# Scattering 48 of the 68 early expert results later: kept in DRAM and scattered in the experts stage, 20 more after the gathers

## The chip, the cores and the metric

The kernel runs on one core of one Trainium2 chip. The metric is device time in microseconds: the median of three runs is 3254.08 us (3247.41 to 3254.96). The execution that was profiled took 3249.84 us, and its trace spans 3248.0 us.

## What is computed

A graph layer on N = 12500 nodes with D = 256 features and E = 212500 edges (sorted by their target), then a layer norm. Cut to what matters here:

```python
h = feats * rsqrt(deg_out)[:, None]
m = segment_sum(h[src], dst) * rsqrt(deg_in)[:, None]
x = m @ W_gc + b_gc + feats @ W_res + b_res
logits = x @ Wg + bg                       # 64 experts, top 2, softmax over the two
for each expert e, its nodes s:            # 256 -> 512 -> 256, gelu
    y[s] += gate * (gelu(x[s] @ w1[e] + b1[e]) @ w2[e] + b2[e])
y = x + y
out = (y - mean) * rsqrt(var + eps) * gamma + beta      # over the nodes
return layernorm(feats + out)                           # over the features
```

## The kernel before

There are four stages, each ended by a barrier over all engines: the columns of the graph and the degrees (to about 350 us of the trace), `aggregate` (to about 2394 us), `experts` (to about 3060 us), and `norms`. Nodes stand in NT = 98 tiles of 128, edges in chunks of 128, PER = 17 chunks to a tile.

**Aggregate** runs in 98 slots, one for a tile. In each, GpSimd (POOL) gathers the source rows of the slot's chunks from `h_table`, one indirect DMA of 128 rows for each chunk, 15 of 17 (L1582); the other two come from `x_ahead` by a plain DMA of SyncE's queue (SP). TensorE (PE) multiplies each chunk with a one-hot matrix into PSUM (L2154), and at fixed chunk numbers k of the slot does the steps of earlier tiles: the product with the weights (k = 3), ranks (13), turning (15), listing the places (16). POOL may be up to 24 chunks ahead of PE. VectorE (DVE) makes the one-hots and does the routing arithmetic.

From slot 63 to slot 96 each slot also computes two **early sets** (jobs 0 to 67): 128 nodes of one expert whose rows are complete in the first 56 tiles. For a job, SP loads the expert's weights (`load_expert`, 1,152 KB in four DMAs, L1425 to L1428), POOL gathers the 128 rows (`fetch_job`, L1556), and PE turns them and computes the hidden layer and the output: for the slot's first job at k = 0, 4 and 8, for its second at k = 8, 11 and 15. `keep_job_turned` (L1812) on DVE copies the turned rows that the hidden layer's matmuls (L2081) wait for. `finish_job` on DVE adds the bias to the output (L1819), makes the gate (L1820, L1822), scales into a ring buffer `eys` of EY = 6 results (L1828), and adds it to a total (L1830). Then POOL scatters the result into `picked` (`send_job`, L1565), each node's two expert results in DRAM.

What sets the order is each engine's own program. DVE's program of slot s ends with: `finish_job` of the slot's first job, `add_x1`, `add_beta` of tile s - 2 (L1650), `finish_job` of its second job; then slot s + 1 begins with routing (L1683 to L1714) and `keep_job_turned` of the first job. SP's program of slot s: a row of `x_ahead`, small columns for later jobs (L1415), weights of the first job of slot s + 1, then `load(s)`, which first waits for `add_beta(s - 2)` (`keep_x_beta`, L1382) and for the landing of what it stored (L1389), another row of `x_ahead` (L1393), in slots with s % 7 = 2 a clearing of part of `picked` (L1403, 1,792 KB) and a store of seven tiles of x1 (L1434, 903 KB), in slots with s % 7 = 6 a load of `m_base` (903 KB), and last the weights of the second job of slot s + 1.

**Experts** runs one turn for each remaining set of 128 nodes, 160 turns in this data. PE's turn is the hidden layer (L2442), turning the next rows (L2435) and the output (L2449). POOL's turn is one scatter of a result (`send`, L2305), which waits for DVE's scaled result (L2382), and one gather of the rows four turns on (`fetch`, L2298). At its start ACT's queue brings 56 tiles of x1 back into `acc3` (L2289), whose space the jobs had used.

## Time and profile before

| | us |
|---|---|
| runs | 3247.41, 3254.96, 3254.08; median 3254.08 |
| the profiled execution | 3249.84 |
| its span in the trace | 3248.0 |
| granted TensorE clock, mean | 0.935 of full speed |
| PE, PEld, DVE busy | 2667.9, 2037.5, 2056.3 |
| ACT, POOL busy | 1243.7, 2108.0 |

PE's busy time is its matmuls with modelled ends, PEld the weight loads beside them. An engine that is busy 82% of the span need not be what the time waits for, and one that is busy 65% may be: POOL's indirect DMAs have a fixed gap between them that counts as idle. What bounds a stage is read in that stage. The page's chain of work that ended last goes back only to the last stage, so it says nothing about the two stages that the change touches; these are read by the timeline and the waits.

### The profile page before, as it was taken

What the parts mean: (1) busy time and instruction counts of PE and PEld (TensorE: products, weight loads), DVE (VectorE), ACT (ScalarE), POOL (GpSimd) and SP (SyncE); (2) the same over time, 40 slices, a digit from 0 to 9 for tenths busy, and PEclk for the clock granted to TensorE, in tenths of its full rate; (3) what the DMA queues carried; (4) which work ended last, traced back from release to release, by engine and by line L of the source; (5) the groups of instructions that cost most, each with busy time, mean ns of one, the idle gap of its engine ahead of it and who ended that gap; (6) DMA issues with size and microseconds to landing.
All of it is one profiled execution on the core that took longest, in us unless ns stands there. A gap on an engine that the chain in (4) does not pass through costs nothing. (4 is left out here: it accounts for less than half of the span.)

```text
span 3248.0 us, 60035 instructions
## 1 busy us (share of the span) xinstructions
PE 2667.9 (82%) x14992; PEld 2037.5 (63%) x14993; DVE 2056.3 (63%) x7118; ACT 1243.7 (38%) x2934; POOL 2108.0 (65%) x2142
## 2 busy tenths in 40 slices
PE   4751689999999899888898989888959999999650
PEld 3541456565666566555776767676748888889640
DVE  7993356666666566666666666666655555555698
ACT  5991122222232232232433334333324444444339
POOL 6887677777777777777777777777714554555300
PEclk9885899999999999999999999999979999999885
DMA  8559545455554654556878787786766555554477
GB/s 259 158 177 342 183 138 180 146 177 188 149 177 144 191 178 143 181 171 188 256 240 255 239 252 242 241 261 214 235 231 189 175 182 181 187 174 138 148 290 248
DMA packets 415795, 653.48 MB, mean 201 GB/s; under 512 B 70847, under 2 KB 307165, under 8 KB 413938
## 3 DMA queue, kind: packets, MB, share of 16 engines
q1 hardware_dynamic: 299790, 355.25, 33.3%
q0 software_dynamic: 101712, 273.85, 28.3%
q10 hardware_dynamic: 14100, 22.04, 1.9%
q8 instruction: 93, 1.52, 0.2%
q14 instruction: 100, 0.82, 0.1%
HBM read 515.73 MB, written 139.19 MB: 202 GB/s over the span
## 5 line engine op out<-in xcount | busy, mean ns | idle before, releaser
L1582 POOL DMA_INDIRECT work<-h_table,src_cols x1452 | 1383.5, 953 | 453.9 <-issue 428.1
L2154 PE MATMUL ps<-work 128*128 128x257 f32 x3322 | 999.5, 395 | 132.0 <-DMA work<-h_table,src_cols 124.3
L2154 PEld LDWEIGHTS ps<-work 128*128 128x128 f32 x3322 | 574.3, 192 | 387.4 <-issue 262.4
L2305 POOL DMA_INDIRECT picked<-ys,places x160 | 170.7, 1067 | 269.1 <-DVE ys L2382 247.5
L1982 PE MATMUL ps<-none_w,none 128*128 128x512 bf16 x879 | 335.6, 382 | 0.0
L2442 PEld LDWEIGHTS ps<-xst,work 128*128 128x128 f32 x2560 | 310.8, 193 | 27.4 <-issue 17.8
L2442 PE MATMUL ps<-xst,work 128*128 128x128 f32 x2560 | 315.5, 277 | 12.6 <-issue 11.9
L2449 PE MATMUL ps<-work,hid 128*128 128x256 f32 x1280 | 307.5, 383 | 2.1 <-ACT hid L2284 1.0
L2284 ACT ACTIVATE hid<-ps,b_cols 128x128 f32<-128x128 f32 x640 | 218.2, 367 | 117.7 <-PE ps L2442 86.7
L2449 PEld LDWEIGHTS ps<-work,hid 128*128 128x128 f32 x1280 | 231.2, 191 | 35.8 <-ACT hid L2284 10.4
L1607 DVE TENSOR_TENSOR work<-rel_cols,ps 128x1152 f32<-128x1152 f32 x196 | 250.5, 1279 | 3.8 <-PE ps L2154 3.7
L1654 DVE TENSOR_TENSOR logits<-ps,gate_bias 128x64 f32<-128x64 f32 x98 | 22.0, 225 | 344.6 <-ACT acc L1489 344.6
L2298 POOL DMA_INDIRECT ring<-x_rows,rows_at x162 | 158.0, 975 | 100.2 <-issue 45.2
L1485 ACT ACTIVATE acc<-acc,f_in 128x256 f32<-128x256 f32 x98 | 49.9, 509 | 382.8 <-DVE f_in L1638 382.8
L1509 ACT ACTIVATE work<-work,f_ahead 128x256 f32<-128x256 f32 x182 | 92.8, 510 | 266.5 <-DMA work<-x_ahead 266.5
L878 ACT ACTIVATE stairs<-iota_f,work 128x128 bf16<-128x128 f32 x624 | 182.6, 399 | 6.0 <-PE ps L955 5.8
L1489 ACT COPY acc<-ps 128x256 f32<-128x256 f32 x98 | 36.5, 372 | 367.2 <-PE ps L2020 362.0
L2093 PE MATMUL ps<-acc 128*128 128x256 f32 x544 | 131.8, 385 | 42.4 <-ACT acc L1516 42.4
L2279 ACT COPY xs<-ring 128x256 f32 (+1 forms) x162 | 65.6, 405 | 250.7 <-POOLq L2325 243.9
L2397 DVE TENSOR_TENSOR ysum<-ps,work 128x256 f32<-128x256 f32 x160 | 68.0, 425 | 134.8 <-PE ps L2449 134.6
L2093 PEld LDWEIGHTS ps<-acc 128*128 128x128 f32 x544 | 100.7, 190 | 67.8 <-ACT acc L1516 55.3
L2081 PEld LDWEIGHTS ps<-acc 128*128 128x128 f32 x1088 | 134.4, 195 | 10.5 <-issue 7.1
(374 smaller groups left out, 5055.4 us busy)
## 6 DMA issues: line engine op xcount, KB each, us to landing
acc<-in_L_gnn_w_dram SPq DMA_DIRECT2D x136, 512.0 KB
work<-in_L_gnn_w_dram SPq DMA_DIRECT2D x128, 512.0 KB
picked<-work SPq DMA_DIRECT2D x14, 1792.0 KB
work<-x_ahead SPq DMA_DIRECT2D x182, 128.0 KB
pk<-picked SPq DMA_DIRECT2D x13, 1792.0 KB, 10.0
work<-h_table,src_cols POOLq DMA_INDIRECT x1452
acc<-m_base SPq DMA_DIRECT2D x14, 903.0 KB, 6.6
x_beta<-xr_x SPq DMA_DIRECT2D x98, 128.0 KB, 2.2
```

What stands on the lines that cost most here:

```text
L878: mm = nc.scalar.activation(stairs[:, k, n, :], iota_f[:, :], ACT.Sign, scale=-1.0, bias=lo_half[:, bass.ds(g * PIECES + 2 * WHOLE + n, 1)])
L1582: pool.indirect_dma_start(out=got[:, c % RING, 0:D], out_offset=None, in_=h_table[:, :], in_offset=bass.IndirectOffsetOnAxis(ap=src_cols[: ...
L1607: nc.vector.tensor_tensor(hot[:, (2 * t + h) % HOTS, 0:b - a, :], rel_cols[:, a:b].unsqueeze(2).broadcast_to([P, b - a, P]), lanes.unsquee ...
L1982: nc.tensor.matmul(ps[:, 7, :], none[:, :], none_w[:, :], start=False, stop=False)
L2081: mm = nc.tensor.matmul(ps[:, 4, h * P:(h + 1) * P], ew1[:, j % EW, k, h * P:(h + 1) * P], exst[:, k, :], start=(k == 0), stop=(k == KD - 1))
L2093: mm = nc.tensor.matmul(ps[:, 5, 0:D], ehid[:, h, :], ew2[:, j % EW, h, :], start=(h == 0), stop=(h == KH - 1))
L2154: mm = nc.tensor.matmul(ps_flat[:, bank(t, k, w[0])], hot[:, (2 * t + (k >= HALF)) % HOTS, k % HALF if k >= HALF else k, :], got[:, c % RI ...
L2284: nc.scalar.activation(hid[:, h, :], ps[:, h, 0:SUP], ACT.Gelu, bias=b1_cols[:, h, bass.ds(e, 1)]).then_inc(h_set, 1)
L2298: pool.indirect_dma_start(out=ring[:, u, :], out_offset=None, in_=x1_rows[:, :], in_offset=bass.IndirectOffsetOnAxis(ap=rows_at[:, u:u + 1 ...
L2305: pool.indirect_dma_start(out=picked[:, :], out_offset=bass.IndirectOffsetOnAxis(ap=places[:, u:u + 1], axis=0), in_=ys[:, u, :], in_offse ...
L2442: mm = nc.tensor.matmul(ps[:, h, 0:SUP], w1s[:, u, k, h * P:(h + 1) * P], xst[:, k, :], start=(k == 0), stop=(k == KD - 1))
L2449: mm = nc.tensor.matmul(ps[:, 4, 0:D], hid[:, h, :], w2s[:, u, h, :], start=(h == 0), stop=(h == KH - 1))
```

## The change

The results of the 68 jobs are no longer scattered between the gathers. Jobs 0 to 47 (`KEPT`) are stored by SP into a new DRAM table `y_jobs`, two per slot, at the end of SP's slot: the first job of the slot before, and the second job of two slots before. In the experts stage they are loaded back in six DMAs of ACT's queue, and POOL scatters one of them per turn in turns 8 to 55 (`send_kept`). The results of jobs 48 to 67 (`SENT_LAST` = 20) stay in SBUF, in `acc3` tiles 56 to 75 whose rows have been stored by then, and POOL scatters them after the last gather. The ring `eys` is 4 results instead of 6, and DVE's scaling waits for the store of the result four jobs before (`ey_out`) instead of the scatter of six jobs before (`ey_sent`). The tiles of x1 come back in 17 DMAs instead of 8: four from ACT's queue (tiles 50 to 55, and in three parts tiles 56 to 75, which held the late results), and from SP's queue twelve of four tiles and one of two, after the kept results that stood there were scattered. For this SP's loop over the experts' weights is unrolled, and so are 14 rounds of POOL's.

```diff
+y_jobs = nc.dram_tensor("y_jobs", [KEPT * P, D], F32).ap()
...
-        EW, ER, EY, EC = 3, 4, 6, JOBS
+        EW, ER, EY = 3, 4, 4
...
+        def y_of(j):
+            return eys[:, j % EY, :] if j < KEPT else acc3[:, COUNTED + j - KEPT, 0:D]
...
+                def store_job(j):
+                    if j >= KEPT:
+                        return
+                    sp.wait_ge(ey_set, j + 1)
+                    if j >= 2:
+                        sp.wait_ge(ey_out[j % 2], 16 * (j // 2))
+                    sp.dma_start(by_lane(y_jobs)[:, j, :], y_of(j)).then_inc(ey_out[j % 2], 16)
...
                     for j in jobs_in(slot + 1)[1:]:
                         load_expert(j)
+                    for j in jobs_in(slot - 1)[0:1]:
+                        store_job(j)
+                    for j in jobs_in(slot - 2)[1:]:
+                        store_job(j)
...
                     if c in fetch_at:
                         fetch_job(fetch_at[c])
-                    if c in send_at:
-                        send_job(send_at[c])
...
+                pool.wait_ge(zeros_out, 16 * SETS)
+                for j in range(KEPT, JOBS):
+                    send_job(j)
+                pool.wait_ge(ey_sent, 16 * SENT_LAST)
...
-                    if j >= EY:
-                        dve.wait_ge(ey_sent[j % 2], 16 * ((j - EY) // 2 + 1))
-                    nc.vector.tensor_scalar(eys[:, j % EY, :], eysum, egate[:, 1:2], None, ALU.mult).then_inc(ey_set, 1)
+                    if EY <= j < KEPT:
+                        dve.wait_ge(ey_out[j % 2], 16 * ((j - EY) // 2 + 1))
+                    elif j == KEPT:
+                        dve.wait_ge(rows_out, stored_to(COUNTED + SENT_LAST))
+                    nc.vector.tensor_scalar(y_of(j), eysum, egate[:, 1:2], None, ALU.mult).then_inc(ey_set, 1)
...
-                with sp.Fori(0, X // U - 1) as i:
+                for i in range(X // U - 1):
                     weights_ahead(i, U)
+                    q = i - QUADS_BARE
+                    if 0 <= q < KEPT_QUADS:
+                        for u in range(R):
+                            sp.wait_ge(kept_sent[u], 16 * (q + 1))
+                        x1_again(sp, *FREED[q + 1])
+                    if q == KEPT_QUADS - 1:
+                        x1_again(sp, *FREED[0])
...
-                for g in range(COUNTED // GT):
-                    act.dma_start(acc3[:, g * GT:(g + 1) * GT, :], by_lane(x1_rows)[:, g * GT:(g + 1) * GT, :]).then_inc(x1_back, 16)
+                for j in range(0, KEPT, PIECE):
+                    act.dma_start(kept[:, j:j + PIECE, :], by_lane(y_jobs)[:, j:j + PIECE, :]).then_inc(kept_in, 16)
+                for a, b in UNUSED:
+                    x1_again(act, a, b)
...
+                def send_kept(n, q, u):
+                    if n == 0:
+                        pool.wait_ge(kept_in, 16 * (KEPT // PIECE))
+                    if q > 0:
+                        pool.wait_ge(kept_sent[u], 16 * q)
+                    pool.indirect_dma_start(out=picked[:, :], out_offset=bass.IndirectOffsetOnAxis(ap=kept_columns[:, n, 1:2].bitcast(I32), axis=0),
+                                            in_=kept[:, n, :], in_offset=None, bounds_check=PLACES - 1,
+                                            oob_is_err=False).then_inc(kept_sent[u], 16)
...
                         if u < fetches:
                             fetch(u)
+                        if kept_quad is not None:
+                            send_kept(R * kept_quad + u, kept_quad, u)
```

SP in aggregate, one slot without a clearing, from `keep_x_beta` to the end of the slot; before:

```order
L1382 DMA x_beta<-xr_x 128x256 [waits any_gathered9]
L1389 DMA xr_x<-in_x_dram 128x256 [waits any_gathered12]
L1393 DMA work<-x_ahead 128x256 [waits any_turns_begun]
L1422 TENSOR_LOAD acc [waits hist_done_any]
L1425 ISA
L1425 DMA acc<-in_L_gnn_w_dram 128x2x512
L1426 DMA acc<-in_L_gnn_w_dram 128x4x256
L1427 ISA
L1427 DMA acc<-in_L_gnn_b_dram 128x256
L1428 ISA
L1428 DMA acc<-acc 128x4
L1393 DMA work<-x_ahead 128x256 [waits any_turns_begun]
```

and of the change (here the slot's end is the two stores, and the names in the brackets are of semaphores that share a number with others: `halves_set_any` is `ey_set`, `risen_set_any` and `col_counted_any` are `ey_out` of even and odd jobs):

```order
L1409 DMA xr_x<-in_x_dram 128x256 [waits any_gathered13]
L1413 DMA work<-x_ahead 128x256 [waits any_gathered0]
L1450 TENSOR_LOAD acc [waits hist_done_any]
L1453 ISA
L1453 DMA acc<-in_L_gnn_w_dram 128x2x512
L1454 DMA acc<-in_L_gnn_w_dram 128x4x256
L1455 ISA
L1455 DMA acc<-in_L_gnn_b_dram 128x256
L1456 ISA
L1456 DMA acc<-acc 128x4
L1443 DMA y_jobs<-acc 128x256 [waits risen_set_any,halves_set_any]
L1443 DMA y_jobs<-acc 128x256 [waits col_counted_any,halves_set_any]
```

The two stores to `y_jobs` stand behind the four DMAs of the weights of the next slot's second job.

DVE in aggregate, `add_beta` and `finish_job` of the second job of slot 65 (job 5); before:

```order
L1650 TENSOR_TENSOR xr_x<-xr_x,ag_beta_b 128x256 [waits any_hot_set]
L1819 TENSOR_TENSOR acc<-ps,acc 128x256 [waits halves_set_any,consts_set,hot_used_any]
L1820 TENSOR_TENSOR acc<-acc 128x1
L1822 SCALAR_TENSOR_TENSOR acc<-acc 128x1 [waits stairs_ready_any]
L1828 TENSOR_SCALAR acc<-acc 128x256 [waits hist_done_any,stairs_ready_any]
L1830 TENSOR_TENSOR acc<-acc 128x256 [waits halves_set_any]
L1720 TENSOR_TENSOR code_diag<-ident,ahead_hi 128x256 [waits f_turned_any]
L1683 SCALAR_TENSOR_TENSOR junk,rt_rank<-iota_f,picks,ps 128x64 [waits ranked]
```

and of the change:

```order
L1677 TENSOR_TENSOR xr_x<-xr_x,ag_beta_b 128x256 [waits any_summed]
L1846 TENSOR_TENSOR acc<-ps,acc 128x256 [waits halves_set_any,consts_set,hot_used_any]
L1847 TENSOR_TENSOR acc<-acc 128x1
L1849 SCALAR_TENSOR_TENSOR acc<-acc 128x1 [waits stairs_ready_any]
L1857 TENSOR_SCALAR acc<-acc 128x256 [waits col_counted_any,hist_done_any,stairs_ready_any]
L1859 TENSOR_TENSOR acc<-acc 128x256 [waits halves_set_any]
L1747 TENSOR_TENSOR code_diag<-ident,ahead_hi 128x256 [waits f_rows_set_any]
L1710 SCALAR_TENSOR_TENSOR junk,rt_rank<-iota_f,picks,ps 128x64 [waits ranked]
```

The order is the same; the scaling (L1828, now L1857) of job 5 has a new wait for the store of an odd job (`col_counted_any`), and stands right behind `add_beta` (L1650, now L1677). Before, this semaphore was that of the scatters, waited for from job 6 on.

POOL in experts, the first turns before (scatters L2305, gathers L2298):

```order
L2305 DMA picked<-ys,places 25088x256 [waits paced,tiles_set_any]
L2298 DMA ring<-x_rows,rows_at 128x258
L2305 DMA picked<-ys,places 25088x256 [waits zero_set,tiles_set_any]
L2298 DMA ring<-x_rows,rows_at 128x258
L2305 DMA picked<-ys,places 25088x256 [waits paced,hot_used_any,tiles_set_any]
L2298 DMA ring<-x_rows,rows_at 128x258
```

and from turn 8 of the change on (L2357 is `send`, L2350 `fetch`, L2377 `send_kept`; `f_out_set_any` is `kept_in`):

```order
L2357 DMA picked<-ys,places 25088x256 [waits paced,hot_used_any,tiles_set_any]
L2350 DMA ring<-x_rows,rows_at 128x258
L2377 DMA picked<-acc 25088x256 [waits f_out_set_any]
L2357 DMA picked<-ys,places 25088x256 [waits zero_set,hist_done_any,tiles_set_any]
L2350 DMA ring<-x_rows,rows_at 128x258
L2377 DMA picked<-acc 25088x256
L2357 DMA picked<-ys,places 25088x256 [waits paced,hot_used_any,tiles_set_any]
```

From turn 8 on a third indirect DMA follows the other two.

## Rows read from the trace of the kernel before

**Rows 1.** Windows: start:end us, length, busy us, clock, DMA share, GB/s.

```profile
1597.21:2125.14 527.93, 473.69 (x2533) 375.65 (x2531) 340.26 (x1281) 196.15 (x396) 400.96 (x417) 0.99 0.80 250
2125.14:2337.28 212.14, 191.97 (x1026) 151.75 (x1024) 134.94 (x513) 81.96 (x164) 161.26 (x168) 0.99 0.76 239
2440.00:3050.00 610.00, 587.98 (x3961) 537.56 (x3961) 335.39 (x1278) 269.78 (x764) 310.46 (x305) 1.00 0.54 169
```

**Rows 2.** Groups of POOL, 1597.21 to 2125.14: busy, mean ns, idle before.

```profile
L1582 POOL DMA_INDIRECT work<-h_table,src_cols x329 | 314.2, 955 | 100.2 <-issue 96.9 <-PE ps L2154 2.1 <-DVE acc L1828 1.2
L1565 POOL DMA_INDIRECT picked<-acc x44 | 44.7, 1015 | 13.4 <-issue 13.4
L1556 POOL DMA_INDIRECT acc<-x_early,acc x44 | 42.7, 970 | 13.4 <-issue 12.8 <-DVE acc L1828 0.6
```

**Rows 3.** Waits, 1597.21 to 2125.14: total us, times, longest.

```profile
PE ps L2154 <- DMA work<-h_table,src_cols: 20.0, 17, 3.8
```

**Rows 4.** Timeline of PE, two slots: start us, us, what, idle before.

```profile
1802.23 1.95 PE L2081 MATMUL ps<-acc 128*128 128x128 f32 x16
...
1815.65 1.99 PE L2093 MATMUL ps<-acc 128*128 128x256 f32 x8 [1.61 <-ACT acc L1516]
...
1824.69 1.95 PE L2081 MATMUL ps<-acc 128*128 128x128 f32 x16
```

**Rows 5.** Timeline of DVE around the same slot's end.

```profile
1814.42 0.42 DVE L1650 TENSOR_TENSOR xr_x<-xr_x,ag_beta_b 128x256 f32<-128x256 f32 x1
1817.68 0.42 DVE L1819 TENSOR_TENSOR acc<-ps,acc 128x256 f32<-128x256 f32 x1 [2.85 <-PE ps L2093]
...
1818.46 0.46 DVE L1828 TENSOR_SCALAR acc<-acc 128x256 f32<-128x256 f32 x1
...
1823.62 0.42 DVE L1812 COPY acc<-ps 128x256 f32<-128x256 f32 x1
```

**Rows 6.** Timeline of SP's queue there.

```profile
1814.87 0.36 SPq L1382 DMA_DIRECT2D x_beta<-xr_x  x1
...
1818.77 0.41 SPq L1425 DMA_DIRECT2D acc<-in_L_gnn_w_dram  x1
...
1820.41 0.53 SPq L1428 DMA_DIRECT2D acc<-acc  x1
```

**Rows 7.** DMA queues, 1818.5 to 1826.5: packets, MB, share of 16 engines.

```profile
q1 hardware_dynamic: 1383, 1.45, 57.0%
```

**Rows 8.** Timeline of DVE, slot 79.

```profile
1935.90 0.35 DVE L1828 TENSOR_SCALAR acc<-acc 128x256 f32<-128x256 f32 x1
```

**Rows 9.** Timeline of SP's queue, slot 79.

```profile
1942.53 1.38 SPq L1428 DMA_DIRECT2D acc<-acc  x1
```

**Rows 10.** Timeline of PE, slot 80.

```profile
1954.95 2.02 PE L2081 MATMUL ps<-acc 128*128 128x128 f32 x16 [0.51 <-DMA acc<-acc]
```

**Rows 11.** Windows: two slots, and the start of the experts.

```profile
1761.15:1789.44 28.29, 22.91 (x117) 17.90 (x115) 15.53 (x59) 8.92 (x18) 21.58 (x23) 0.94 0.89 290
1789.44:1811.89 22.45, 20.85 (x117) 16.95 (x115) 15.55 (x59) 8.92 (x18) 16.97 (x19) 1.00 0.80 253
...
2405.00:2408.00 3.00, 2.17 (x9) 1.78 (x10) 0.61 (x2) 0.40 (x1) 0.94 (x1) 0.50 0.98 362
2408.00:2411.00 3.00, 3.00 (x15) 2.91 (x15) 0.24 (x1) 1.41 (x4) 0.94 (x1) 0.50 1.01 401
```

**Rows 12.** DMA issues by line: KB each, median us to landing.

```profile
acc<-m_base SPq DMA_DIRECT2D x14, 903.0 KB, 6.6
x_beta<-xr_x SPq DMA_DIRECT2D x98, 128.0 KB, 2.2
```

**Rows 13.** Timeline of POOL in the experts.

```profile
2605.13 1.00 POOL L2305 DMA_INDIRECT picked<-ys,places  x1 [1.37 <-DVE ys L2382]
2606.44 0.98 POOL L2298 DMA_INDIRECT ring<-x_rows,rows_at  x1 [0.30 <-issue]
```

**Rows 14.** Timeline of POOL between the stages.

```profile
2397.85 0.99 POOL L2298 DMA_INDIRECT ring<-x_rows,rows_at  x1 [41.32 <-DVE rows_at L2358]
```

More of the change, by code:

```diff
@@ L43 @@
 PER_SLOT = 2
+JOBS = PER_SLOT * (JOB_LAST - JOB_FIRST + 1)
+SENT_LAST = 20
+KEPT = JOBS - SENT_LAST
+KEPT_TILE = 2
+QUADS_BARE = 2
+KEPT_QUADS = KEPT // 4
 GT = 7
@@ L1479, in _ @@
                 sp.wait_ge(rows_out, 16 * (ALL_IN + SETS - 1 + SET))
+                for n in range(2):
+                    sp.wait_ge(ey_out[n], 16 * ((KEPT + 1 - n) // 2))
             @block.scalar
@@ L2186, in _, with experts @@
                 list_places(NT - 1)
[L2189 removed]
+def experts(nc, x1_rows, y_jobs, picked, w1s, w2s, b2s, w_in, load_weights, ident, ones, table, base_of, from_of, b1_cols, y_total, acc3, ps, N, D, X, H, KD, KH, ROW, PLACES):
     with ExitStack() as part:
@@ L2237, in experts, with x1_again @@
         x1_back = sem2("x1_back")
+        kept_in = sem2("kept_in")
+        kept_sent = [sem2(f"kept_sent{u}") for u in range(R)]
+        kept = acc3[:, KEPT_TILE:KEPT_TILE + KEPT, 0:D]
+        kept_columns = job_columns(acc3, D + 1)
+        PIECE = 8
+        assert KEPT % PIECE == 0 and KEPT % R == 0 and QUADS_BARE + KEPT_QUADS <= (X - 1) // R
+        assert KEPT_TILE + KEPT <= COUNTED and U == R
+        def x1_again(eng, a, b):
+            eng.dma_start(acc3[:, a:b, :], by_lane(x1_rows)[:, a:b, :]).then_inc(x1_back, 16)
+        FREED = [(0, KEPT_TILE)] + [(KEPT_TILE + R * q, KEPT_TILE + R * (q + 1)) for q in range(KEPT_QUADS)]
+        UNUSED = [(KEPT_TILE + KEPT, COUNTED)] + [(t, min(t + GT, COUNTED + SENT_LAST)) for t in range(COUNTED, COUNTED + SENT_LAST, GT)]
+        PARTS_BACK = len(FREED) + len(UNUSED)
         def bounds(engine, e, more=0):
@@ L2331, in quad @@
                             fetch(u)
-                quad(0)
-                with pool.Fori(1, whole) as j:
+                        if kept_quad is not None:
+                            send_kept(R * kept_quad + u, kept_quad, u)
+                for j in range(QUADS_BARE):
+                    quad(j)
+                for q in range(KEPT_QUADS):
+                    quad(QUADS_BARE + q, kept_quad=q)
+                for u in range(R):
+                    pool.wait_ge(kept_sent[u], 16 * KEPT_QUADS)
+                with pool.Fori(QUADS_BARE + KEPT_QUADS, whole) as j:
                     quad(j)
```

53 lines of the change are left out of this document (25 added, 28 removed).

## Prediction

> **What bounds the kernel now.** The page's chain of the work that ended last stays in the last stage, so I read the stages of the change one by one: first the busy times in windows, then the groups and waits of the engine that looks full, then timelines of one slot on every engine that hands something on.
>
> In the slots with jobs, POOL looks only three quarters busy: 401.0 of 527.9 us in the 22 slots from 1597.21 to 2125.14, 24.0 us a slot [rows 1]. But its idle time is put down to "issue", 0.30 us ahead of each indirect DMA, and to hardly anything else [rows 2]: it issues without a break. A gather takes 0.955 + 0.30 = 1.26 us, a scatter 1.015 + 0.30 = 1.32 us, a fetch 1.28 us; 15 gathers, two fetches and two scatters make 24.1 us. So POOL sets the pace on average. PE is close behind. In a slot where it waits for no gather it comes round in 22.46 us (the hidden layer of the first job starts at 1802.23 and again at 1824.69 [rows 4]), and its waits for gathers are 20.0 us in all of the 22 slots [rows 3]. What POOL gives up is worth at most the distance from 24.0 to about 22.5 us.
>
> PE's own round hangs on DVE at one point. DVE scales the second job's result at 1818.46, then does its routing, and at 1823.62 copies the turned rows of the next job, until 1824.04 [rows 5]. PE's hidden layer starts at 1824.69 [rows 4]. A stop of DVE at the scaling is therefore covered for 0.65 us, and the rest of it reaches PE whole.
>
> In the experts POOL has room. 305 indirect DMAs in 610 us are 152.5 turns of 4.00 us, PE is busy 96% of them [rows 1], and POOL waits 1.37 us of a turn for DVE's result [rows 13].
>
> **Part 1, scatters leave the gathers.** Two scatters of 1.32 us fall out of a slot, so POOL needs 24.1 - 2.6 = 21.5 us. That is below PE's 22.46, so PE is the bound unless something else stops it. All 68 scatters are 90 us of POOL, of which PE leaves about 1.4 us a slot to be had.
>
> **Part 2, the new wait on DVE.** Here I expect the change to lose. For odd jobs, the store that the scaling of job j waits for (job j - 4, the second of two slots before) is issued at the end of SP's program of the very slot in which DVE scales job j. SP gets there only after `keep_x_beta`, and that waits for `add_beta`, the instruction that stands right ahead of `finish_job` in DVE's program, as the order above shows. So each time the store has yet to be issued when DVE is ready. What lies between is read from one slot. `add_beta` starts at 1814.42 [rows 5], SP stores x_beta at 1814.87, starts the weights at 1818.77 and issues their last DMA at 1820.41 [rows 6]. Only then come the two stores, 256 KB behind 1,152 KB of weights in the same queue. From 1818.5 to 1826.5 that queue moved 1.45 MB [rows 7], which is the weights and two rows of x_ahead and little more, so I take the weights to be in at about 1826.5. That is 8.0 us after DVE's scaling would have started at 1818.46; the 256 KB of the stores at the same rate of 0.18 MB/us or somewhat faster add about 0.9. The stall is about 9.0 us, estimated.
>
> The trace has no store behind weights, so I bound it. From below: the stores land as quickly after their own issue as those of x_beta do, 2.2 us [rows 12]. They are issued by about 1820.41 + 0.53 + 2 x 0.4 = 1821.7, landed by 1823.9, a stall of 5.4 us. From above: 11 us, with the queue as slow as 1.45 MB in 8 us for all 1.41 MB of weights and stores, from 1820.0 on, and 1.5 us of other traffic. I take 9.0, nearer to the slot that was read, and because of the second place.
>
> That place is slot 79, one of four slots in the range (65, 72, 79, 86) where a clearing of 1,792 KB and a store of 903 KB go ahead of the weights. There DVE scaled at 1935.90 [rows 8], the last DMA of the weights was issued at 1942.53 [rows 9], and PE's hidden layer had to wait for it until 1954.95 [rows 10]: the small DMA took 12.4 us, since it stood behind the rest. The stall would be 1954.95 - 1935.90 + 0.9 = 19.9 us. In slots 69, 76 and 83 a load of m_base goes ahead; it lands in 6.6 us where 128 KB take 2.2 [rows 12], so up to 4.4 us more, of which I take half.
>
> The Trainium skill ("DMA: Bandwidth & Descriptors", section "Queues, rings and completion order") says that descriptors of one ring are taken in order but that a later one may finish its write before an earlier one, while the semaphore's increment comes after all earlier writes of that DMA engine. By the first half of that alone the stores could overtake the weights, by the second their landing could not be seen before. The 12.4 us of slot 79 agree with the second.
>
> The wait is there for jobs 5, 7, ... 47, the second jobs of slots 65 to 86: 22 slots. Even jobs wait for a store issued a slot earlier, which has landed, and late jobs (48 on) have no such wait. The round of a stalled slot is: from PE's hidden layer to DVE's scaling, 1818.46 - 1802.23 = 16.2; the stall; from the scaling to the end of the copy, 1824.04 - 1818.46 = 5.6, and 0.1 to PE's start. Together 21.9 us + stall.
>
> Behind DVE's wait stand the routing of the next slot and the copy; behind the copy PE, and behind PE the one-hots' release and POOL, which stops at 24 chunks ahead. PE idles about 8 us in each such slot. Its clock then falls: in the slot that held a 3.8 us wait (the longest of rows 3) the granted clock was 0.94 and PE was busy 22.91 us, against 20.85 in the slot after it at 1.00 [rows 11]. So a fall to the lower of its two levels (1.2 GHz of 2.4) cost 2.1 us. From above: at the start of the experts, after a long idle time, it was at 0.50 in two windows of 3 us in a row [rows 11], which costs 3 us or a little over. From below 0, if the lost time is hidden in waits for DVE. I take 2.2 a slot.
>
> Sum for the 22 slots: 18 x (21.9 + 9.0 + 2.2) = 596; 4 x (21.9 + 19.9 + 2.2) = 176; 3 x 2.2 = 7; together 779 us, against 527.9 [rows 1]: +251.
>
> **Part 3, the slots after.** From 2125.14 to 2337.28 there are nine slots, 23.6 us each [rows 1]. Without stall and with POOL ahead they go at PE's pace, about 22.6: -9 us. Slots 63 and 64 ran at 22.5 already.
>
> **Part 4, the 20 late scatters.** 20 x 1.32 = 26 us on POOL after the last gather. POOL is up to 24 chunks, some 30 us, ahead of PE there, and after its last scatter it idled 41.3 us until the experts began [rows 14]. 0, from -1 to +3.
>
> **Part 5, experts.** A third indirect DMA makes POOL's turn 1.00 + 0.98 + 1.0 and three gaps of 0.3 [rows 13]: 3.9 us against the mean turn of 4.00. It just fits, but short turns no longer do; 48 turns x 0.1 = +5 us, from 0 to +15. The kept results (6 MB at the stage's start; at the 401 GB/s of rows 11 that is 16 us) are in before turn 8, some 33 us into the stage, and loading x1 from SP's queue (516 KB every four experts) lies in a stage whose DMA share is 0.54 [rows 1]: 0.
>
> **Sum.** 3249.84 (the profiled execution's own time, 4 us under the median of the runs) + 251 - 9 + 0 + 5 = 3497 us.
>
> **Rivals.**
> - *The stores overtake the weights.* Stall 5.4 us, and in the four slots 1942.53 + 1.38 + 0.8 + 2.2 - 1935.90 = 11.0. 18 x 29.5 + 4 x 35.1 = 671, +144; in all 3390 us. For it: x_beta's 2.2 us. Against it: the weights of slot 79, landed 12.4 us after issue [rows 9, 10]. 7%. This is also what the first half of the Trainium skill's rule would give ("DMA: Bandwidth & Descriptors", same section), were the increment not held back.
> - *POOL becomes the bound of the experts as well.* If the third DMA delays the fetch and every one of the 48 turns takes a whole DMA more, 48 x 1.3 = 62 instead of 5: 3554 us. For it: 3.9 against 4.00 leaves nothing. Against it: DVE's result is what POOL waits for now, 1.37 us in a turn. 6%.
> - *No stall: faster.* If SP reached the stores before DVE's scaling, POOL's relief would be seen and PE would bound: 22 x 22.6 = 497 against 528, -31 - 9 + 5: 3215 us. The point from which it decides is a landing within 0.65 us after DVE's scaling. For it: POOL is without a break now, and 90 us leave it. Against it: SP's 1820.41 stands behind DVE's 1818.46 and before the stores. 5%.
>
> My forecast holds 80%, and 2% is left for no change. A measurement of this kernel can tell about 0.3%, 10 us, from none. Slower by more than that: the forecast, the first two rivals and a little, 93%; faster 5%; the same 2%.
>
> The range: with a stall 1 us shorter and a clock that costs 0.5 us, 22 x 2.7 = 59 less, 3438; some way to the first rival, 3405. With 1.5 us more of stall and 3.4 for the clock, 22 x 2.7 = 59 more, 3556; I say 3560.
>
> **What would show it.** In the profile of the changed kernel, the waits list DVE's scaling <- DMA y_jobs 22 times, about 240 us in all, longest near 20; PE's L2081 line (the hidden layer of the first job) waits for DVE's copy some 22 times; POOL waits for PE; the clock over these slots is below 0.95. The stretch of 22 slots is some 779 us. If POOL's idle time is still "issue" alone and the slots take 22.5 us, step 2 is wrong and the third rival right. If stalls are near 5 us it is the first. If the experts are over 20 us longer it is the second.

## The result and the profile after

The changed kernel takes 3521.17 us (median of 4 runs, 3516.01 to 3524.79); the kernel before, beside it, 3252.49 us (4 runs, 3247.41 to 3254.96). The ratio is 1.082, 95% interval 1.0807 to 1.0833. The prediction was 3497 us, range 3405 to 3560. The profiled execution took 3516.01 us, with a span of 3514.0 us and a mean granted clock of 0.902 of full speed (before 3248.0 us and 0.935).

First the two windows that answer to the first two of [rows 1]: 22 slots, then nine.

```profile
1597.19:2370.18 772.99, 511.64 (x2510) 416.87 (x2530) 336.11 (x1277) 196.21 (x396) 363.48 (x381) 0.84 0.56 173
2370.18:2577.29 207.11, 188.64 (x1018) 153.54 (x1024) 135.04 (x518) 81.84 (x164) 147.12 (x154) 0.98 0.76 234
```

POOL's busy time fell from 401.0 to 363.5 us (fifth pair of numbers), as it should with the scatters gone; DVE's and ACT's stayed. PE did the same work in 511.6 busy us instead of 473.7, at a clock of 0.84 instead of 0.99, and the stretch grew from 527.9 to 773.0 us. Apart from PE and its weight loads (38 and 41 us more), no engine is busier in the added 245 us. The waits of that stretch (total us, times, longest) say for whom everybody stands still:

```profile
POOL acc L1592 <- DVE acc L1857: 295.0, 43, 13.7
DVE acc L1857 <- DMA y_jobs<-acc: 243.8, 22, 18.3
PEld ps L2110 <- DVE acc L1839: 233.8, 22, 17.9
PE ps L2110 <- DVE acc L1839: 224.9, 22, 17.5
```

L1857 is DVE's scaling (before: L1828), L1839 the copy of the turned rows (L1812), L2110 the hidden layer (L2081), L1592 the fetch of a job's rows (L1556). This is one chain: DVE waits for the store into `y_jobs`, PE for DVE's copy behind it, and POOL for DVE's scaling, since the fetch of job j needs the buffer whose rows job j - 4 used up. In POOL's groups of the stretch, to be held against [rows 2], the fetch has the new wait, and the scatter's group is gone:

```profile
L1610 POOL DMA_INDIRECT work<-h_table,src_cols x337 | 318.7, 946 | 110.2 <-issue 101.8 <-PE ps L2183 8.4
L1592 POOL DMA_INDIRECT acc<-x_early,acc x44 | 45.6, 1037 | 295.3 <-DVE acc L1857 295.0 <-issue 0.3
```

One slot shows it in time. DVE, the same place as [rows 5]:

```profile
1707.86 0.42 DVE L1677 TENSOR_TENSOR xr_x<-xr_x,ag_beta_b 128x256 f32<-128x256 f32 x1
...
1711.67 0.22 DVE L1849 SCALAR_TENSOR_TENSOR acc<-acc 128x1 f32<-128x1 f32 x1
1720.70 0.35 DVE L1857 TENSOR_SCALAR acc<-acc 128x256 f32<-128x256 f32 x1 [8.81 <-DMA y_jobs<-acc]
...
1725.80 0.41 DVE L1839 COPY acc<-ps 128x256 f32<-128x256 f32 x1
```

SP's queue in the same slot [rows 6]:

```profile
1708.31 0.35 SPq L1402 DMA_DIRECT2D x_beta<-xr_x  x1
...
1711.73 0.42 SPq L1453 DMA_DIRECT2D acc<-in_L_gnn_w_dram  x1
...
1713.84 0.65 SPq L1456 DMA_DIRECT2D acc<-acc  x1
1714.59 1.00 SPq L1443 DMA_DIRECT2D y_jobs<-acc  x2
```

And PE [rows 4]:

```profile
1717.61 0.70 PE L2183 MATMUL ps<-work 128*128 128x257 f32 x2
1726.27 3.78 PE L2110 MATMUL ps<-acc 128*128 128x128 f32 x16 [7.95 <-DVE acc L1839]
```

`add_beta` (L1677) releases the store of x_beta 0.03 us after its end; four DMAs of weights follow, and the two result stores (L1443) are issued only at 1714.59, when DVE has been ready to scale since 1711.89. They land at 1720.7, 5.1 us after the second of them was issued. PE idles for 7.95 us, and then its 16 matmuls take 3.78 us where before they took 1.95: they run at half speed, at the lower of the clock's two levels (1.2 GHz of 2.4).

In the experts, ScalarE's start of the stage (ACTq is DMA issue by ACT's queue), before:

```profile
2394.47 4.12 ACTq L2289 DMA_DIRECT2D acc<-x_rows  x8
...
2404.59 0.40 ACT L2279 COPY xs<-ring 128x256 f32<-128x256 f32 x1 [4.46 <-POOLq L2314]
```

and after:

```profile
2629.87 15.46 ACTq L2339 DMA_DIRECT2D acc<-y_jobs  x6
2645.35 5.14 ACTq L2276 DMA_DIRECT2D acc<-x_rows  x4
...
2651.93 0.39 ACT L2329 COPY xs<-ring 128x256 f32<-128x256 f32 x1
```

Six loads of kept results keep ACT's queue for 15.46 us, ahead of the copy that PE's first matmul needs. POOL issues the first fetch at 2633.24, and PE begins 19.1 us later (7.2 before):

```profile
2633.24 0.99 POOL L2350 DMA_INDIRECT ring<-x_rows,rows_at  x1 [32.74 <-DVE rows_at L2426]
```

```profile
2652.37 0.69 PE L2503 MATMUL ps<-ident,xs 128*128 128x128 f32 x2 [32.37 <-ACT xs L2329]
```

POOL before had two DMAs in a turn [rows 13]; now there are three (L2377 is the kept scatter):

```profile
2746.24 0.98 POOL L2357 DMA_INDIRECT picked<-ys,places  x1 [0.33 <-issue]
2747.52 0.98 POOL L2350 DMA_INDIRECT ring<-x_rows,rows_at  x1 [0.30 <-issue]
2748.81 0.99 POOL L2377 DMA_INDIRECT picked<-acc  x1 [0.30 <-issue]
2750.77 1.10 POOL L2357 DMA_INDIRECT picked<-ys,places  x1 [0.97 <-DVE ys L2450]
```

To answer to the last window of [rows 1] by parts, the turns 8 to 56 and 56 to 159 of the experts, before:

```profile
2448.57:2642.30 193.73, 185.32 (x1247) 168.87 (x1246) 105.53 (x404) 83.91 (x239) 97.96 (x97) 1.00 0.58 181
2642.30:3053.50 411.20, 394.98 (x2660) 361.06 (x2659) 226.30 (x864) 181.59 (x514) 209.67 (x206) 1.00 0.53 162
```

after:

```profile
2698.02:2904.18 206.16, 187.30 (x1246) 168.66 (x1244) 106.75 (x403) 81.43 (x238) 144.46 (x145) 1.00 0.68 211
2904.18:3319.83 415.65, 395.39 (x2661) 361.32 (x2660) 226.46 (x864) 179.78 (x514) 210.25 (x205) 1.00 0.55 171
```

The whole difference of 266.0 us between the two spans, cut where PE begins a tile's sum and where POOL issues its first fetch and its scatters:

| stretch | before | after | difference |
|---|---|---|---|
| up to slot 63, and slots 63 to 65 | 1597.2 | 1597.2 | 0.0 |
| 22 slots, 66 to 87 | 527.9 | 773.0 | +245.1 |
| 9 slots, 88 to 96 | 212.1 | 207.1 | -5.0 |
| rest of aggregate, to the first fetch | 60.6 | 56.0 | -4.6 |
| first fetch to turn 8 | 50.7 | 64.8 | +14.1 |
| turns 8 to 56 | 193.7 | 206.2 | +12.5 |
| turns 56 to 159 | 411.2 | 415.7 | +4.5 |
| the rest | 194.6 | 194.1 | -0.5 |

### The profile page after: what moved, and what is told of

Its sections match the earlier page's. It is cut to its first block and busy times, and to the rows that moved or that the text cites. A ratio compares the mean times of both kernels' runs of the same rounds, so it can differ in the third digit from the quotient of the medians.

```text
span 3514.0 us, 59487 instructions
## 1 busy us (share of the span) xinstructions
PE 2697.5 (77%) x14863; PEld 2085.0 (59%) x14993; DVE 2053.7 (58%) x7118; ACT 1239.7 (35%) x2934; POOL 2105.9 (60%) x2142
## 5 line engine op out<-in xcount | busy, mean ns | idle before, releaser
L2183 PEld LDWEIGHTS ps<-work 128*128 128x128 f32 x3322 | 587.1, 194 | 332.1 <-issue 211.7
L2110 PE MATMUL ps<-acc 128*128 128x128 f32 x1088 | 173.6, 326 | 231.3 <-DVE acc L1839 224.9
L2510 PE MATMUL ps<-xst,work 128*128 128x128 f32 x2560 | 315.2, 276 | 12.7 <-issue 11.8
L2357 POOL DMA_INDIRECT picked<-ys,places x160 | 168.0, 1050 | 241.6 <-DVE ys L2450 180.3
L2011 PE MATMUL ps<-none_w,none 128*128 128x512 bf16 x815 | 311.5, 382 | 0.0
L2110 PEld LDWEIGHTS ps<-acc 128*128 128x128 f32 x1088 | 167.0, 238 | 242.9 <-DVE acc L1839 233.8
L1592 POOL DMA_INDIRECT acc<-x_early,acc x68 | 69.7, 1024 | 320.0 <-DVE acc L1857 310.9
L2350 POOL DMA_INDIRECT ring<-x_rows,rows_at x162 | 159.8, 987 | 88.5 <-issue 47.1
L1552 ACT ACTIVATE acc<-ps,acc 128x128 f32<-128x128 f32 x272 | 77.5, 368 | 342.9 <-PE ps L2110 342.4
L1857 DVE TENSOR_SCALAR acc<-acc 128x256 f32<-128x256 f32 x68 | 24.3, 357 | 245.4 <-DMA y_jobs<-acc 243.8
```

Of the source, the lines that this page charges most:

```text
L2011: nc.tensor.matmul(ps[:, 7, :], none[:, :], none_w[:, :], start=False, stop=False)
L2110: mm = nc.tensor.matmul(ps[:, 4, h * P:(h + 1) * P], ew1[:, j % EW, k, h * P:(h + 1) * P], exst[:, k, :], start=(k == 0), stop=(k == KD - 1))
L2183: mm = nc.tensor.matmul(ps_flat[:, bank(t, k, w[0])], hot[:, (2 * t + (k >= HALF)) % HOTS, k % HALF if k >= HALF else k, :], got[:, c % RI ...
L2350: pool.indirect_dma_start(out=ring[:, u, :], out_offset=None, in_=x1_rows[:, :], in_offset=bass.IndirectOffsetOnAxis(ap=rows_at[:, u:u + 1 ...
L2357: pool.indirect_dma_start(out=picked[:, :], out_offset=bass.IndirectOffsetOnAxis(ap=places[:, u:u + 1], axis=0), in_=ys[:, u, :], in_offse ...
L2510: mm = nc.tensor.matmul(ps[:, h, 0:SUP], w1s[:, u, k, h * P:(h + 1) * P], xst[:, k, :], start=(k == 0), stop=(k == KD - 1))
```

## Experiments

Each run is compared with runs of the kernel before on the same chip: 3252.76 us for the early store, the ring of six, the stores before the weights and the 30 extra matmuls; 3248.94 for the 42 extra matmuls, the wide rows and the two runs on top of them; 3247.59 for the version of what was learnt and its first variant; 3255.16 for the last. The windows and waits come from one profiled execution of each kernel.

**Is it the wait for the store, and is it the store's place?** The odd jobs' store at the head of SP's next slot, ahead of the loads there, instead of behind the weights of a slot later:

```diff
                         load_weights(sp, 0, 0)
+                    for j in jobs_in(slot - 1)[1:]:
+                        store_job(j)
                     if among(slot + 1):
...
                         store_job(j)
-                    for j in jobs_in(slot - 2)[1:]:
-                        store_job(j)
```

> The changed kernel, with one line moved: SP stores the second job's result at the start of the next slot's program (16 us before DVE needs the room), not at the end of the slot after that. Theory (DVE waits for a store that is issued too late and behind 1,152 KB of weights): the 22 slots, 773 us in the changed kernel, take 22 x 22.5 = 495 us, DVE's wait for y_jobs of 244 us is gone, total 3521 - 278 = 3243 us. Rival (it is the traffic of the stores itself, 256 KB more per slot beside the gathers, that slows the slots): the bytes are the same, so the slots stay above 700 us and the total near 3520. The experts stage stays 31 us longer than before in either case.

3259.85 us (8 runs), ratio 1.0024, interval 1.0013 to 1.0035. Without touching the order of the stores, only the ring back at six results:

```diff
-        EW, ER, EY = 3, 4, 4
+        EW, ER, EY = 3, 4, 6
```

> The changed kernel with a ring of 6 results instead of 4, the stores where they are. Theory: the wait is then for a store that was issued a slot earlier, so the stall is gone although the stores still stand behind the weights: 3243 us, as with the store moved. Rival (the stores' traffic): near 3520. If the place behind the weights cost something apart from DVE's wait, this kernel would be slower than the one with the store moved.

3258.93 us (10 runs), 1.0021, interval 1.0011 to 1.0031. The waits of DVE's scaling (total us, times), of the changed kernel:

```profile
  DMA y_jobs<-acc: 243.8, 22
```

of the early store:

```profile
  DMA y_jobs<-acc: 5.3, 3
```

and none with the ring of six. The 22 slots of the early store:

```profile
1595.40:2108.70 513.30, 466.11 (x2532) 379.48 (x2531) 340.43 (x1287) 198.03 (x398) 368.40 (x385) 0.98 0.82 261
```

513.0 us with the ring of six. Two edits that share nothing but the removed wait give the same, 260 us less. So the wait is the cause, and POOL's relief is real too: 14.6 us under the 527.9 of before, regular slots at 22.5 us as PE's round has it. Both missed the 3243 us that I had expected, though, by 16 to 17 us. From slot 66 to the first fetch both are 28 us shorter than the kernel before, and from there to turn 159 the early store is 32 us longer (36 with the ring of six): the experts take it all back.

**How much of the stall is the weights ahead of the store?** Both stores in front of the second job's weights, still behind `keep_x_beta`:

```diff
-                    for j in jobs_in(slot + 1)[1:]:
-                        load_expert(j)
                     for j in jobs_in(slot - 1)[0:1]:
                         store_job(j)
                     for j in jobs_in(slot - 2)[1:]:
                         store_job(j)
+                    for j in jobs_in(slot + 1)[1:]:
+                        load_expert(j)
```

> The changed kernel with SP's two stores ahead of the next weights instead of behind them, still in the same slot's program after x_beta. Theory: the store is still issued after DVE is ready, but no longer queued behind 1,152 KB: stall 1819.2 + 2.2 - 1818.5 = about 2.9 us in 18 slots, about 10 us in the four with a clearing ahead of it: 92 us instead of 244. With half the clock cost the 22 slots take 22 x 21.9 + 92 + 22 x 1 = 596 us, total 3344 us. If the queue behind the weights did not matter (the stores overtake them), it would be only the 2.3 us of issuing that is saved, 22 x 2.3 = 51 us: 3470.

3395.83 us (4 runs), 1.0443, interval 1.0426 to 1.046. It lies between the two expectations. The waits:

```profile
  DMA y_jobs<-acc: 134.1, 22
```

SP and DVE in the slot that answers to the one shown above:

```profile
1694.84 0.35 SPq L1402 DMA_DIRECT2D x_beta<-xr_x  x1
...
1697.55 1.12 SPq L1443 DMA_DIRECT2D y_jobs<-acc  x2
1699.20 0.42 SPq L1453 DMA_DIRECT2D acc<-in_L_gnn_w_dram  x1
```

```profile
1701.96 0.35 DVE L1857 TENSOR_SCALAR acc<-acc 128x256 f32<-128x256 f32 x1 [3.54 <-DMA y_jobs<-acc]
```

The stores are issued 2.7 us after x_beta instead of 6.3, and DVE goes on 3.3 us after their issue ended instead of 5.1. In this slot 3.6 us of issue and 1.8 of landing are saved, in the slots with large transfers 3 to 4 us in all. Summed over the 22 slots, the changed kernel's 244 us of stall are 102 us from DVE being ready to the end of the stores' issue and 142 us from there to their landing; with the stores ahead of the weights these are 24 and 110 us. So 110 us go when the weights are no longer ahead, 78 of them by earlier issue and 32 by earlier landing. 134 us stay, because the store still waits in SP's program for `add_beta`: it is issued only about when DVE is ready, and nearly its whole landing is then waited for. The 22 slots fell by 120 us for 110 us of stall; the other 10 fit the clock, whose time at the low level fell from 249.2 to 129.7 us.

**What does the low clock cost?** Extra matmuls into an unused place on PE right before it waits, so that it does not stand idle:

```diff
                 def hide_job(j, t):
+                    if j % PER_SLOT == 0 and 6 <= j <= KEPT:
+                        for _ in range(30):
+                            idle_turns()
```

> The changed kernel with 30 idle matmuls (128x512 bf16, 0.216 us each, 6.5 us) that PE runs ahead of its wait in the 22 stalled slots; they add zeros. Theory (the fall of the clock costs 2.2 us of each stalled slot): the granted clock of the 22 slots rises from about 0.84 to 0.95 or more, the slots fall from 773 to about 725 us, total 3473 us. Rival (the stall itself is all, the lower clock hides in waits): total 3521 or, where the idle matmuls outlast a stall, a little more.

3503.32 us (4 runs), 1.0768, interval 1.075 to 1.0786. The time at the low level within the 22 slots fell from 249.2 to 85.3 us, and the slots by 14 us only; the other matmuls ended before the stall did. But the slots where the clock held are the measurement I wanted. Slot 68 of the changed kernel, then of this one (window, then its DVE row):

```profile
1672.06:1705.36 33.30, 23.19 (x117) 18.91 (x116) 15.28 (x59) 8.91 (x18) 16.29 (x17) 0.85 0.55 162
```

```profile
1687.90 0.35 DVE L1857 TENSOR_SCALAR acc<-acc 128x256 f32<-128x256 f32 x1 [9.32 <-DMA y_jobs<-acc]
```

```profile
1673.15:1704.31 31.16, 27.60 (x148) 19.80 (x145) 15.19 (x59) 8.92 (x18) 16.32 (x17) 1.00 0.57 174
```

```profile
1688.98 0.35 DVE L1857 TENSOR_SCALAR acc<-acc 128x256 f32<-128x256 f32 x1 [9.30 <-DMA y_jobs<-acc]
```

The same stall, and 33.30 - 9.32 = 24.0 us against 31.16 - 9.30 = 21.9 us. Six of the slots ran with no low clock, and each is 21.9 us plus its stall. So a round without stall is 21.9 us and the low clock costs 2.1 us a slot.

With 42 of the extra matmuls (`range(42)`):

> The changed kernel with 42 extra matmuls into an unused place (9.1 us at full clock) on TensorE right before it waits for the job's row in each of the slots with the new wait; the wait itself stays. In the run with 30 of them, five slots had no time at the low clock and took 21.9 us plus their stall. Theory A (the slot is the round of 21.9 us plus the stall plus 2.3 us for the low clock): the regular slots with a stall under 10 us fall to 31 us, the low clock's time in the 22 slots falls from 249 us to under 60 us and the 22 slots from 773 us to about 735 us. Rival B (the low clock costs next to nothing, since the DMA sets the slot): the low clock's time falls all the same and the slots stay at 760 us or above, because the store then lands no earlier and the wait grows by what the matmuls gain.

3492.01 us (one run). Over the 22 slots:

```profile
1598.10:2338.10 740.00, 668.18 (x3413) 470.73 (x3455) 334.59 (x1277) 196.18 (x396) 363.39 (x381) 0.98 0.59 181
```

The low clock's time is down to 30.7 us, the stall unchanged (245.9 us), and 33 us are gone. Most regular slots stand at 31.5 us, which is PE's round of 22.46 us [rows 4] and the 9.07 us of extra matmuls: they now last as long as what they cover, so this run understates the clock's price. That the DMA sets the slot and the clock costs nothing is refuted either way.

**Why do ten DMA issues take 20 us?** On top of the early store, kept rows 258 floats wide, so that a lane's eight rows are one stretch of memory:

```diff
-    y_jobs = nc.dram_tensor("y_jobs", [KEPT * P, D], F32).ap()
+    y_jobs = nc.dram_tensor("y_jobs", [KEPT * P, ROW], F32).ap()
...
-        kept = acc3[:, KEPT_TILE:KEPT_TILE + KEPT, 0:D]
+        kept = acc3[:, KEPT_TILE:KEPT_TILE + KEPT, :]
```

> The kernel with the stores moved to the front of SP's order (the previous change), and each kept row is stored 258 floats wide, so that the six reloads ahead of the experts read and write whole stretches of memory instead of pieces of 1 KB. Theory A (the 20.6 us that ScalarE spends on issuing the ten loads before its first copy of the experts come from the many pieces): the six issues fall from 15.5 us to about 5 us, TensorE's first matmul of the experts comes about 8 us after the first fetch instead of 19 us, and the time falls by 10 us, to 3250 us. Rival B (the issues are slow because the loads are large or queued): they still take 15 us and the time stays at 3260 us. The store of a job grows by less than 1%, so the 22 slots stay at 513 us.

3247.58 us (11 runs), 0.9993, interval 0.9984 to 1.0002: no change against the kernel before. ACT's queue:

```profile
2370.94 3.03 ACTq L2339 DMA_DIRECT2D acc<-y_jobs  x6
2374.00 2.06 ACTq L2276 DMA_DIRECT2D acc<-x_rows  x4
```

15.46 us became 3.03 for the same six loads, and PE starts 7.8 us after the first fetch instead of 19.1. It was the many pieces. The four x1 loads behind them fell from 5.14 to 2.06 us with their own pieces unchanged, so the pieces that stand ahead in the queue cost issue time too. But the first eight turns (from the first scatter to the ninth) now take 37.2 us, 4.5 more than before; that they meet the loads is tested below.

**What does the third DMA cost?** On top of that, the kept scatters left out. The 48 results then never reach `picked`, so this kernel serves for the timing alone:

```diff
-                    pool.indirect_dma_start(out=picked[:, :], ...).then_inc(kept_sent[u], 16)
+                    pool.sem_inc(kept_sent[u], 16)
```

> The kernel of the run before, with the scatters of the 48 kept results left out of the experts (their rows are not written; the semaphores are raised on GpSimd at once). Theory A (the third DMA of a turn is what costs in turns 8 to 56, by GpSimd's 1.26 us for each): the 48 turns fall from 205 us to 193.7 us as before the change, so the span is 11 us shorter; turns 0 to 8 and 56 to 159 stay. Rival B (the cost lies in the x1 loads and the load on the DMA queues): the 48 turns stay within 3 us of 205 us.

3237.69 us (one run). And, with the kept scatters in again, SP's x1 loads behind the last weights:

```diff
                 for i in range(X // U - 1):
                     weights_ahead(i, U)
-                    q = i - QUADS_BARE
...
                 weights_ahead(X // U - 1, 1)
+                for a, b in FREED:
+                    x1_again(sp, a, b)
```

> The wide-row kernel with SP's reloads of the x1 rows all issued after the last of the experts' weights instead of among them (one per quad). Theory A (the 4 to 8 us lost in turns 56 to 159, and a part of turns 8 to 56, come from these loads delaying the weights or the fetches): turns 8 to 56 fall by up to 3 us and turns 56 to 159 from 418 us back to 411 us. Rival B (the lag is carried over from the start, or is chance between runs): both stay within 2 us of the run with wide rows.

3242.97 us (one run). The experts by parts, in us from the first fetch on:

| kernel | to turn 8 | 8 to 56 | 56 to 159 | sum |
|---|---|---|---|---|
| before | 50.7 | 193.7 | 411.2 | 655.6 |
| changed | 64.8 | 206.2 | 415.7 | 686.6 |
| wide rows | 55.6 | 208.4 | 415.1 | 679.1 |
| wide rows, no kept scatters | 54.7 | 196.3 | 417.4 | 668.4 |
| wide rows, x1 loads last | 54.4 | 204.5 | 415.6 | 674.6 |
| all together (below) | 55.7 | 195.6 | 413.3 | 664.6 |
| x1 loads early on SP (below) | 49.5 | 211.3 | 412.1 | 672.9 |
| x1 loads later on SP (below) | 50.0 | 199.2 | 424.9 | 674.1 |

48 third DMAs cost 12.1 us (208.4 - 196.3), 0.25 a turn. The x1 loads in turns 8 to 56 cost about 4, by single profiles. Turns 56 to 159 did not come back to 411 us with the loads last, so there theory A fell; the 4 us are not explained. Single profiles may differ by that much; and every kernel here has the unrolled loops of the change, which were not tested apart.

**A version of what was learnt.** Early stores, wide rows, 28 late results instead of 20, and kept scatters in three turns of four:

```diff
-SENT_LAST = 20
+SENT_LAST = 28
-QUADS_BARE = 2
-KEPT_QUADS = KEPT // 4
+QUADS_BARE = 1
+PER_QUAD = 3
+KEPT_QUADS = -(-KEPT // PER_QUAD)
...
-                    elif j == KEPT:
-                        dve.wait_ge(rows_out, stored_to(COUNTED + SENT_LAST))
+                    elif j >= KEPT:
+                        dve.wait_ge(rows_out, stored_to(COUNTED + j - KEPT + 1))
```

and the x1 loads last, as above.

> The kernel with early stores and wide rows, and in addition: 28 results scattered in the drain and 40 kept (28 x 1.28 us = 36 us of GpSimd's 56 us there, of which 32.7 us are still idle with 20), three kept scatters in each group of four turns from turn 4 on, each late result waiting only for its own row's store, and SP's x1 loads after the last weights. Theory (gain of the aggregate stage kept at about 26 us; the start of the experts costs nothing more; a third DMA costs 0.25 us, so 40 of them 10 us; the contention at the start of the experts 4 us; the rest 2 to 5 us): 3242 us, about 7 us or 0.2% below the kernel before the change. Rival (each of the 40 costs more, as they now stand in turns 4 to 60 with the loads of the start still under way, or the extra eight lengthen the drain): 3250 us or more.

3229.85 us (5 runs, 3227.97 to 3237.12), 0.9945, interval 0.9931 to 0.9959: 0.55% faster than the kernel before, and 12 us better than I had expected. (The profiled execution is the slowest of the five.) POOL before the first fetch:

```profile
2353.26 0.97 POOL L1598 DMA_INDIRECT picked<-acc  x1 [0.30 <-issue]
2377.21 1.00 POOL L2348 DMA_INDIRECT ring<-x_rows,rows_at  x1 [22.98 <-DVE rows_at L2424]
```

Eight more scatters eat 10 us of an idle time that was 32.7, and from slot 97 to the first fetch it takes 56.6 us where the wide rows had 56.0: next to nothing is later for it. Turns 8 to 56, with the x1 loads last and a kept scatter in every turn:

```profile
2427.09:2631.62 204.53, 187.79 (x1246) 169.78 (x1244) 107.07 (x403) 82.50 (x238) 144.81 (x144) 0.99 0.64 202
```

and in three turns of four:

```profile
2432.92:2628.55 195.63, 186.60 (x1250) 169.18 (x1249) 107.58 (x405) 83.07 (x240) 133.51 (x132) 1.00 0.64 203
```

9 us less, though 36 of these turns, instead of 48, still have a third DMA: at 0.25 us each, the twelve fewer would be worth 3. My reading, which no run separates from chance between two profiles, is that one free turn of four lets POOL catch up, where in a row without a gap a delay is never made good. PE's waits for the copy of fetched rows over these turns agree with it, first every turn, then three of four:

```profile
PE ps L2500 <- ACT xs L2326: 12.4, 10, 2.8
```

```profile
PE ps L2501 <- ACT xs L2327: 4.5, 7, 0.9
```

**Can the first eight turns be had back?** The x1 loads that ACT issues at the start, one after each group of weights on SP:

```diff
                     weights_ahead(i, U)
+                    if 1 <= i <= len(UNUSED):
+                        x1_again(sp, *UNUSED[i - 1])
...
-                for a, b in UNUSED:
-                    x1_again(act, a, b)
```

> The kernel of the run before with the four or five x1 loads that ScalarE issues ahead of its first copy (some 4.5 MB) moved to SP, one after each of the groups 1 to 5 of the experts' weights. Theory A (turns 0 to 8 take 37 us against 33 us before the change because the fetches share the DMA engines with these loads): turns 0 to 8 fall to 33 to 34 us and the time to 3238 us. Rival B (the same bytes then collide with the weights in turns 8 to 56, or the 4 us come from something else): the sum of turns 0 to 56 stays within 2 us and the time with it.

3240.93 us (11 runs), 0.9981, interval 0.9972 to 0.999: 11 us slower than with the loads at the start. The start fell by 6.2 us, so it was the loads that it met; and turns 8 to 56 grew by 15.7. Theory A was right for the start, and neither it nor rival B for the sum, which grew by 9.5. Then the same five loads at the groups 8 to 12 (`if 8 <= i < 8 + len(UNUSED)`):

> The previous kernel with the same five x1 loads on SP after the groups 8 to 12 of the weights, at about turns 80 to 130, where no kept scatter is left. In that kernel turns 0 to 8 had come down from 38.2 to 32.1 us and turns 8 to 56 up from 195.6 to 211.3 us. Theory A (a load of 0.9 MB costs only where GpSimd also issues a third DMA per turn, since the fetches then have no slack to land late): turns 0 to 8 stay at 32 us, turns 8 to 56 go back to 196 us, the rest grows by at most 2 us, and the time is 3225 us. Rival B (each load costs its 3 us wherever it lies, as the experts' DMAs have no slack anywhere): turns 56 to 159 grow by 10 us or more and the time stays near 3238 us.

3241.56 us (6 runs), 0.9962, interval 0.995 to 0.9975. Turns 8 to 56 are back to 199.2 us, turns 56 to 159 up by 11.6. All five loads lie in the latter, from 2710.8 us on, so the 3.6 us by which turns 8 to 56 stand above 195.6 are none of theirs. The first of the five is 1.8 MB, the others 0.9 MB; taken as six of 0.9 MB they cost 15.7 / 6 = 2.6 us each in the first place and 11.6 / 6 = 1.9 in the second. So the loads cost time where there are no kept scatters too, as rival B has it. How much is less sure: against the kernel before on its own chip this one gains 13.6 us, the one with the loads early on SP 6.7, and the one with the loads at the start 17.7, so by the medians the later place costs 4 to 6 us and not the 9.5 by which the experts grew in the profiles. The first load, and ACT's copy 10 us later:

```profile
2710.82 0.67 SPq L2277 DMA_DIRECT2D acc<-x_rows  x1
```

```profile
2721.14 0.40 ACT L2329 COPY xs<-ring 128x256 f32 x1 [6.26 <-POOLq L2384]
```

This is the longest wait of ACT's copy for POOL's fetch over turns 56 to 159; the totals, with the loads there, then without:

```profile
ACT xs L2329 <- POOLq L2384: 167.8, 96, 6.3
```

```profile
ACT xs L2327 <- POOLq L2384: 162.0, 102, 3.6
```

Behind each of the other four loads a wait of 4.2 to 4.4 us follows within 10 us: the fetched rows land late while such a load is under way. At the start of the stage the same bytes cost 6 us in all, presumably since there much is waited for anyway.

## Why the prediction was right, and where a term was off

**The bounds before: right.** POOL issued without a break and PE was close behind. Without the scatters and without the wait a regular slot takes 22.5 us, as PE's round of 22.46 us in [rows 4] said.

**Part 1, the relief: right in kind, half the size,** 14.6 us in the 22 slots of the early store, where 24.0 - 22.5 gives 33 (the third rival took 31). The mean of 24.0 hid two kinds of slot. The four slots with large transfers and the three slots in the stretch that follow one take 176.4 us together before and 176.5 with the early store: POOL's relief changes nothing there. The other fifteen took 23.4 us before and take 22.5, and that is the whole 14.6. The forecast of the changed kernel did not use this term, since DVE's stall sets its slots.

**Part 2, the wait: right in place, number, chain and sum.** 22 times, 243.8 us, longest 18.3; I had said 22 times, about 240, near 20. The sum was right partly because two errors cancel. The regular stalls are 8.8 to 11.8 us with a mean of 9.8 (I took 9.0, and 2.2 more in three of them: 9.4), the four long ones 15.5 to 18.3 with a mean of 16.7 (I took 19.9 from one slot). For the stores themselves I added 0.9 us to the regular stall, though at the rate of 0.18 MB/us that I name they take 1.4; with that, the slots without any large transfer come to 9.5, which is what they measure. In the long ones I gave the stores the 12.4 us that a small DMA of slot 79 took to land; the stores landed 5.7 to 8.6 us after their issue. The round without a stall is 21.9 us, exactly as worked out from the cover of 0.65 us, and the clock costs 2.1 us a slot (I took 2.2). 22 x 21.9 + 243.8 leaves 47 us of the 773.0, 2.15 a slot. The forecast for this stretch was 779.

The first rival, stores that overtake the weights, fails in the trace: the stall was 8.81 us where it asked for 5.4, since the stores landed 5.1 us after their issue and not 2.2. Taking the weights away is a weaker proof than its 110 us look, for the rival would save the earlier issue too, and only 32 us are earlier landing. In the Trainium skill ("DMA: Bandwidth & Descriptors", section "Queues, rings and completion order") the second half of the rule, that an increment comes after a DMA engine's earlier writes, is what these runs agree with: the same store lands 5.1 us after its issue behind weights and 3.3 without them. That descriptors are taken in order would delay it as well, and no run here tells the two apart.

**Part 3, the nine slots: -5.0** for a forecast of -9; with the early store it is -8.6.

**Part 4, the late scatters: no cost, as said,** but the stage's rest came out 4.6 us shorter, outside my -1 to +3. All changed kernels of this study have 56 to 57 us there, against 60.6 before; what shortens it was not tested.

**Part 5, the experts: mis-sized.** I gave +5, from 0 to +15; measured are +31, outside that range. Three pieces of it were found. The kept loads I had priced at nothing, by their bytes: 6 MB that are in before turn 8. Their bytes were not the question, but their issue, 15.46 us on ACT's own queue ahead of its first copy, +11.9 to PE's start; the wide rows took that away. The third DMA I took at 0.1 us a turn from the mean (3.9 us against 4.00); it costs 0.25, probably because turns vary and a full engine does not catch up. The x1 loads I took at nothing since the DMA share was 0.54; the small ones here cost about 4 us together, and 0.9 MB cost 2 to 3 us in the later kernels. The 4.5 us of turns 56 to 159 stay open. The condition I named for the second rival, experts over 20 us longer, was met, yet its mechanism, a whole DMA more in each turn (62 us), was not what happened.

**The third rival, no stall,** stood at 3215 us. With the stall taken out, the kernel stands at 3260, 7 us slower than before, not 35 faster: its 31 us in the slots were 14.6, and its +5 in the experts +32.

The profiled execution lies 19 us above the forecast: Part 5 makes +26, Part 3 +4, the 22 slots -6 and Part 4 -5. The median lies another 5 us above. So the loss, its place and its mechanism were foreseen. The total came within 1% although one part missed by 26 us, because the one large term was right to 6 us; that the errors inside that term nearly cancel was luck.

## What to carry to other kernels

When work is moved off a full engine, look at where its buffers are now released, and count what stands ahead of that release in the program and the queue that do it: here another place of the store in SP's order, or two more buffers of 128 KB, were worth 260 us. Price a DMA that is issued from a compute engine's queue by its pieces and not by its bytes. An engine that just fits its turn on average may not fit: here 48 full turns in a row took 204.5 us, and 195.6 with one in four left free. And do not take the mean distance between two engines for the gain: look at which slots the relief can shorten at all.

## What the runs showed of the hardware that was not expected

- Issuing six loads of 1 MB kept ACT's queue for 15.46 us with rows of 1 KB and 3.03 us with whole stretches; four unchanged loads behind them took 5.14 and 2.06 us to issue.
- 0.9 MB of a large load among loads of weights lengthened the experts by 2.6 us in one place and 1.9 in another (single profiles), at a DMA share of 0.58 to 0.66; a wait for a gather under way grew to 6.3 us.
